# In a four-layer transformer kernel, the second mixing stage applies its projection's layer norm on the scalar engine and adds it to x in one vector operation per group

## What is computed

```python
    def _layernorm(x, axis=-1, eps=1e-05):
        m = jnp.mean(x, axis=axis, keepdims=True)
        v = jnp.var(x, axis=axis, keepdims=True)
        return (x - m) / jnp.sqrt(v + eps)
    ...
        y = (num / den).transpose(0, 2, 1, 3).reshape(b, t, HEADS * HD)
        return y @ Wo.T
    ...
    x = x + _layernorm(_L1_attn_ref(_layernorm(x, axis=-1), ...), axis=-1)
    x = x + _layernorm(_L1_ffn_ref(_layernorm(x, axis=-1), ...), axis=-1)
```

## Time and profile before

| | us |
|---|---|
| three runs | 2811.05, 2815.23, 2816.77 |
| median | 2815.23 |
| profiled execution | 2811.87 |
| span of its trace | 2810.2 |

### The profile page before, as it was taken

How to read it: one execution, slowest core, us unless ns; L and a number is a source line. 1 busy time by engine, 2 the same in 40 slices (tenths; PEclk the granted TensorE clock), 3 DMA queues, 4 the chain that set the end, 5 groups by cost and what they waited for, 6 DMA issues and landing times. The chain is left out here.

```text
span 2810.2 us, 57154 instructions
## 1 busy us (share of the span) xinstructions
PE 2453.4 (87%) x15239; PEld 1160.4 (41%) x15239; DVE 2196.9 (78%) x5740; ACT 1769.2 (63%) x2700; POOL 561.3 (20%) x644
## 2 busy tenths in 40 slices
PE   5887999999999999678999997994999999996756
PEld 3442333333333333254666665653233333333545
DVE  6897989898989999286777767996666676666968
ACT  2452666666666666317777756884787888873546
POOL 1453111111111111240000000222222222222300
PEclk9996999999999999799999998997999999998979
DMA  5985353535453533360000002555877777764503
GB/s 178 282 274 136 76 103 85 104 84 103 85 103 85 104 84 83 96 170 1 0 0 0 0 0 76 179 186 177 161 143 145 149 140 145 142 136 117 152 1 119
DMA packets 224106, 309.46 MB, mean 110 GB/s; under 512 B 32416, under 2 KB 170352, under 8 KB 211952
## 3 DMA queue, kind: packets, MB, share of 16 engines
q1 hardware_dynamic: 223616, 307.47, 45.4%
q10 hardware_dynamic: 432, 1.31, 0.2%
HBM read 181.29 MB, written 126.88 MB: 110 GB/s over the span
## 5 line engine op out<-in xcount | busy, mean ns | idle before, releaser
L941 ACT ACTIVATE a_p<-psum 128x1024 f32<-128x1024 f32 (+1 forms) x640 | 567.3, 942 | 304.3 <-PE psum L1039 304.1
L941 ACT ACTIVATE b_p<-psum 128x512 f32<-128x512 f32 (+2 forms) x640 | 444.2, 750 | 148.3 <-PE psum L1039 145.3
L993 DVE CUSTOM_DVE_ANT_0 a_dump<-psum,a_bias 128x128 bf16<-128x128 f32 (+3 forms) x1024 | 447.0, 488 | 59.5 <-PE psum L1028 51.9
L991 DVE TENSOR_REDUCE a_peak<-psum 128x1 f32<-128x512 f32 x512 | 334.3, 687 | 25.0 <-PE psum L1028 21.9
L970 DVE COPY b_twin<-psum 128x512 f32<-128x512 f32 (+1 forms) x320 | 203.7, 636 | 168.3 <-PE psum L1039 164.9
L1039 PE MATMUL psum<-b_qs,b_ks 96*128 96x512 bf16 (+3 forms) x1536 | 307.9, 330 | 31.2 <-DMA b_vs<-values 31.2
L1055 PE MATMUL psum<-b_p,b_vs 128*32 128x512 f32 (+3 forms) x3072 | 314.7, 497 | 6.3 <-POOL b_p L913 6.2
L913 POOL TENSOR_SCALAR_AFFINE_SELECT a_p<-a_p 128x512 f32<-128x512 f32 x256 | 162.3, 634 | 754.2 <-ACT a_p L941 742.4
L1028 PE MATMUL psum<-a_ks,a_qs 96*128 96x128 bf16 (+2 forms) x1008 | 274.5, 333 | 27.1 <-DMA a_vs<-values 18.6
L913 POOL TENSOR_SCALAR_AFFINE_SELECT b_p<-b_p 128x512 f32<-128x512 f32 x256 | 159.4, 634 | 444.4 <-DVE b_p L973 433.2
L1039 PE MATMUL psum<-a_qs,a_ks 98*128 98x512 bf16 x1008 | 234.8, 328 | 9.8 <-DMA a_qs<-a_rows 3.8
(11 more groups left out here) (197 smaller groups left out, 3652.5 us busy)
## 6 DMA issues: line engine op xcount, KB each, us to landing
qk_parts<-l_parts SPq DMA_DIRECT2D x96, 256.0 KB, 3.1
qk_parts<-g_parts SPq DMA_DIRECT2D x96, 256.0 KB, 2.8
values<-l_vx SPq DMA_DIRECT2D x64, 256.0 KB, 3.3
sums<-a_osb SPq DMA_DIRECT2D x64, 256.0 KB, 2.3
m_num<-sums SPq DMA_DIRECT2D x64, 256.0 KB, 3.8
m_inv<-reciprocals SPq DMA_DIRECT2D x64, 256.0 KB, 4.5
values<-g_vx SPq DMA_DIRECT2D x64, 256.0 KB, 3.0
sums<-b_osb SPq DMA_DIRECT2D x64, 256.0 KB, 2.3
```

The source lines that it names most:

```text
L941: act.activation(p[s % SLOTS][:, 2 * k:2 * k + heads, cols], m.psum[:, at:at + heads, cols], ACT.Exp if softmax else ACT.Square, scale=z.D ...
L991: last = dve.tensor_reduce(dst, piece, AX.X, ALU.max)
L993: last = dve.tensor_tensor_reduce(dump[c % SRING][:, at:at + w], piece, bias[:, 512 - w:], 1.0, NEG, ALU.add, ALU.max, dst)
```

## The change

In the second call only (`flipped` given), `add` is replaced by three functions. `shifts` on VectorE takes the reciprocal and minus mean times reciprocal. `scaled` on ScalarE waits for it and writes projection times scale plus shift from PSUM into a new double-buffered tile `part`, with four activations. `add_part` on VectorE waits for that and adds `part` to x in one operation. L1229 and its table update go, as the mean is now in x. `divide` on GpSimd waits for `add_part` of three groups before in place of L1229's semaphore, `project` for `scaled` of two groups before in place of L1224. The order on VectorE and on ScalarE changes as the last lines of each part show.

```diff
+            def shifts(i, u):
+                n = 2 * i + u
+                inverse(dve, sd[u], rs[u], sd_ready, rs_ready, n)
+                dve.scalar_tensor_tensor(out=moved[u][:, :], in0=mv[u][:, :, 0], scalar=-1.0, in1=rs[u][:, :],
+                                         op0=ALU.mult, op1=ALU.mult).then_inc(moved_ready, 1)
+
+            def add_part(i, u):
+                n = 2 * i + u
+                dve.wait_ge(part_ready, n + 3)
+                x = m.x[:, bass.ts(n, G), :]
+                dve.tensor_tensor(x, x, part[u][:, :, :], ALU.add).then_inc(added, 1)
+
             def measure_x(i, u):
                 n = 2 * i + u
-                wait_alone(dve, added, n + 3, m.alone)
+                wait_alone(dve, added, n + 4, m.alone)
...
-                streamed(dve, GROUPS, (1, add), (1, measure_x), (0, measure), (1, divisor), (3, largest))
+                streamed(dve, GROUPS, (1, shifts), (0, measure), (1, add_part), (1, measure_x), (3, largest), (1, divisor))
...
-                pool.wait_ge(shift_ready, n + 1)
+                pool.wait_ge(shift_ready if flipped is None else added, n + 1)
...
+            def scaled(i, u):
+                n = 2 * i + u
+                act.wait_ge(moved_ready, n + 1)
+                act.wait_ge(added, n + 2)
+                for t, bank in enumerate(banks(u)):
+                    last = act.activation(part[u][:, t, :], bank, ACT.Identity, bias=moved[u][:, t:t + 1],
+                                          scale=rs[u][:, t:t + 1])
+                last.then_inc(part_ready, 1)
...
-                streamed(act, GROUPS, (1, root_x), (0, root), (1, inner), (2, take_turned))
+                streamed(act, GROUPS, (1, scaled), (0, root), (1, root_x), (1, inner), (2, take_turned))
...
-                pe.wait_ge(added, n + 1)
+                pe.wait_ge(added if flipped is None else part_ready, n + 1)
```

More of the change, by code:

```diff
@@ L1133, in mix_pass @@
             raw2, mv2, sd2, rs2 = sb("raw2", [P, G, 6]), sb("mv2", [P, G, 2]), sb("sd2", [P, G]), sb("rs2", [P, G])
-            offset, xn = sb("offset", [P, G]), sb("xn", [P, G, z.D])
-            (raw2_done, mv2_ready, sd2_ready, rs2_ready, offset_ready, xn_ready, turned, flipped_ready) = sems(
+            offset, xn, part = sb("offset", [P, G]), sb("xn", [P, G, z.D]), sb("part", [P, G, z.D])
+            (raw2_done, mv2_ready, sd2_ready, rs2_ready, offset_ready, xn_ready, turned, flipped_ready,
+             part_ready) = sems(
                 nc, *["m_" + x for x in ("raw2_done", "mv2_ready", "sd2_ready", "rs2_ready", "offset_ready",
-                                         "xn_ready", "turned", "flipped_ready")])
+                                         "xn_ready", "turned", "flipped_ready", "part_ready")])
         block = ctx.enter_context(nc.Block())
@@ L1197, in _ @@
         def _(dve):
-            dve.sem_inc(added, 2)
+            dve.sem_inc(added, 2 if flipped is None else 3)
             dve.sem_inc(shift_ready, 3)
@@ L1274, in _ @@
                 act.sem_inc(flipped_ready, 2)
+                act.sem_inc(part_ready, 2)
+            def scaled(i, u):
[6 more added lines that the diff above has]
+                last.then_inc(part_ready, 1)
             def root(i, u):
```

## The result

The changed kernel takes 2858.24 us (median of 4 runs, 2857.72 to 2859.64); the kernel before, beside it, 2814.53 us (2811.05 to 2816.77). The ratio is 1.0161, interval 1.0148 to 1.0173: slower by 1.6%, or 43.7 us. The forecast was 2859.5 us, 44.3 above the median it started from.

A forecast was written before the change was run, and what follows sets the result against it. VectorE was taken to bound the stage at 7.43 us a step; the change closes a 10.22 us path. Steps +41.9, head +1.8 and tail +0.6 make +44.3 on 2815.2: 2859.5 us, range 2848 to 2872.

The forecast's parts named there:

- VectorE sets the pace before: In the stage of the kernel before, VectorE is busy 100.53 of 108.85 us and sets the 7.43 us step.
- The closed path: Through ScalarE and VectorE, one group's scaled to take_turned must end before the next scaled: 10.22 us a step against 7.43.
- Head, steps and tail: In the changed stage: head +1.8 us, 15 steps +41.9, tail +0.6, together +44.3 us.
- What was said to be hidden: In the stage, measure (1.84 us) under the wait for scaled, and TensorE's projection (3.7 us within some 8), nearly free.
- ScalarE would never be idle before scaled: Sign in the changed stage: ScalarE idles before root_x and inner, never before scaled; otherwise the prediction is wrong.
- (a): Rival: in the stage VectorE stays the bound and gives back 0.44 us a step, about -6 us, 2809 us; chance 0.05.
- (b): Rival: ScalarE is free when moved comes; the handover stalls 0.41 us a step, eating the saving, 2815 us; chance 0.03.
- The rule of the Trainium skill: For the stage: improve the highest-occupancy engine first, moving work to ScalarE where VectorE is saturated; so the change gains.
- (c): Rival: the closed path holds and the addition collides with GpSimd's multiply, up to 2.34 us each, 2894 us; chance 0.03.
- (d): Rival: the change doesn't do what it says, for instance another link hides scaled; near 2815 us; chance 0.01.

The follow-up runs named there:

- the first opened version: Changed kernel with the addition and all behind it one group later, GpSimd's multiply released by the addition of four groups before: 2832.58 us, ratio 1.0081.

## Why the prediction was right

**VectorE sets the pace before.** It held: with 4 more activations on ScalarE the step stayed 7.4, and a reserved tile and another order left the time where it was. Of the two runs with the activations one matched the kernel before, the other lay 0.3% above it, with the old step in its trace.

**The closed path and its sum.** The forecast put it at 10.22 us a step; measured are 10.27 and 10.32 by turns. Link by link, in the timeline above: part to addition 2.08 (2639.71 to 2641.79; forecast 1.93 + 0.12), addition to statistics 1.37 (1.22 + 0.15), statistics to aggregation 1.55 (1.55), to the reduction 0.33 (0.30), to the reciprocal 1.13 (1.14), to the offset 0.20 (0.20), to inner 0.31 (0.30), to take_turned 1.98 (1.98), to part 1.32 (1.33). No link is off by more than 0.03. That the path, and not the amount of work, sets the time is shown by the runs that took a link out, shortened one, did both, or lengthened one: 8.95, 9.64, 8.31 and 11.27 us, each within 0.1 of its sum.

**Head, steps and tail.** From the attention pass's last matmul to the first statistics of x 33.3 us against 31.4, +1.9 (forecast +1.8; there `moved` met GpSimd's multiply once more and took 1358 ns). The 15 steps 151.27 us (150.7), +42.4 (+41.9). The tail is 11.06 us against 10.49, +0.6 (+0.6). Together +44.9, forecast +44.3. That the head agrees to 0.1 is partly luck: in the other versions that leave it alone it was between 32.2 and 33.8 us. So is a median within 1.3 us of the forecast, when executions of the kernel before beside it scatter by 5.7; the step is what the sum can be held to. The rest of the span's +45.8 is +2.8 in the passes ahead and -1.9 in the one behind, which the change doesn't touch and which lie within what such runs scatter.

**What was said to be hidden.** It was, but less comfortably than written. At its slower pace TensorE's projection took 6.75 us in some steps (3.72 in others), and VectorE waited for it 8 times, 10.2 us in all, where I had named no such wait. In the steps it lay under `part`: in the timeline above the measurement behind the slow projection was done at 2640.17, `part` at 2641.62. So no step was longer for it: the step with the slow projection (from 2631.42, granted clock 0.54) took 10.27 us, the next, with the fast one (from 2641.68, granted clock 1.00), 10.32. The windows of the two projections, columns as in the earlier trace rows:

```profile
2631.42:2638.17 6.75, 6.75 (x16) 5.09 (x16) 4.76 (x14) 2.19 (x6) 2.35 (x1) 0.54 0.20 57
2641.68:2645.40 3.72, 3.71 (x16) 2.95 (x16) 3.32 (x10) 0.40 (x2) 2.30 (x1) 1.00 0.00 0
```

Two figures of the prose don't follow from its own links: scaled begins 3.6 us after the offset (0.30 + 1.98 + 1.33), not 3.3, and ends at 5.5; and a multiply would have to be released some 6.7 us after the end of an addition to meet the next one, not 5. Neither enters the sum. The idle times came out as 3.3 us before root_x (forecast 2.9), 1.3 before inner (1.1) and mostly 1.5 to 3.4 before the addition (3). That ScalarE would never be idle before scaled was too strict a sign: it was, once, 1.6 us at the first group, where it has nothing else to do yet. That GpSimd had waited for VectorE "in every step" was loosely put: 12 times of 16 by the earlier trace rows.

**The rivals.** (a) and (b), which needed ScalarE to be free when `moved` is ready, didn't come; the wait of `part` for `moved`, once in 16, says why. The rule of the Trainium skill that spoke for (a), Perfetto Trace Analysis, section Identifying the Most-Contended Engine, picked the right engine, and that engine did get 7 us of work less in the window; the trace shows that this gave no time. (c) didn't occur, and forced it costs 26 us. (d) fell as the links came out one by one. A rival that I hadn't named, that the lower clock of TensorE makes part of the 42 us, falls with the two steps just compared.

## What to carry to other kernels

Before moving a step to an engine with room, write down the queue order of both engines and look for a path that leaves the step, goes through the other engine, and comes back to the same queue ahead of the next group's step: its length is the new period, however idle both engines look. Such a path is shortened link by link, by putting independent work of another group into its waits, and opened only by a lag of one more group; then look for the next path, through the banks that the moved step frees. And count what is left to win first: here an open order got back the 44 us, and the single addition, worth 0.44 us a step on paper, was mostly eaten by the gaps of the longer pipeline, its head and its tail.

## What the runs showed of the hardware

Two operations of 128x1024 that both read two inputs from the core's memory, VectorE's addition (1.22 us) and GpSimd's multiply (2.34 us), don't share: started 0.07 us apart the later one, the addition, took 3.35 us. Four activations of 128x256 out of PSUM took 1.91 us and eight of 128x128 took 2.88, so halving the width saves only about a quarter of an activation's spacing. TensorE's granted clock over the stage fell from 0.89 to 0.76 as its busy share fell from 68% to 61%. Its 16 matmul instructions of a group took 3.72 us at a granted clock of 1.00 (2.4 GHz) and 6.75 at 0.54, most of it at the lower level, 1.2 GHz. That had no effect on the step of the changed kernel, where the waits for it ended before `part` did, and cost, by estimate, 1.5 to 3 us in every other step of the first opened version, where VectorE did and the projection took 5.2 to 6.8 us.
